# A causal attention layer on one core: masking the keys of each half of the heads on GpSimd in place of VectorE

## What is computed

```
qp = q @ Wq.T ;  kv = latent_kv @ Wkv_expand.T ;  k, v = split(kv)
qh, kh, vh = heads of qp, k, v          # 16 heads of 16 channels
scores = einsum('bhqd,bhkd->bhqk', qh, kh) / sqrt(16)
scores = where(causal, scores, finfo.min)
out = einsum('bhqk,bhkd->bhqd', softmax(scores), vh)
return out @ Wout.T
```

## Time and profile before

| what | us |
|---|---|
| median of 3 runs | 1821.97 (1820.47 to 1822.61) |
| the profiled execution, its own time | 1817.92 |
| its span, first to last instruction | 1816.1 |
| TensorE busy | 1622.1 (89%) |
| VectorE busy | 1230.1 (68%) |
| ScalarE busy | 742.8 (41%) |
| GpSimd busy | 921.1 (51%) |

### The profile page before, as it was taken

The page is one execution under the profiler, slowest core; times in us unless marked ns, Lnnn a source line. Parts: engine busy times, 40 slices in busy tenths (PEclk is TensorE's granted clock), DMA queues, the critical chain, the costliest instruction groups (busy, mean ns, idle before and its releaser), DMA issues. The chain is left out here.

```text
span 1816.1 us, 27644 instructions
## 1 busy us (share of the span) xinstructions
PE 1622.1 (89%) x8770; PEld 1110.5 (61%) x8770; DVE 1230.1 (68%) x2197; ACT 742.8 (41%) x1965; POOL 921.1 (51%) x799
## 2 busy tenths in 40 slices
PE   5999977999999999999999996799999289978980
PEld 4667744555555555555555553499999167665870
DVE  5598768777787777777787744466666757756433
ACT  3100102444444444444444452466666156652220
POOL 0377747777888777777888452023332000000636
PEclk9999987999999999999999997699999699988895
DMA  6434344122212221222212002664444420001443
GB/s 199 134 67 96 69 106 136 42 79 79 79 41 75 79 70 52 79 78 79 79 39 77 10 11 87 211 196 130 132 139 116 156 58 1 0 4 37 123 112 108
DMA packets 91472, 157.41 MB, mean 87 GB/s; under 512 B 45841, under 2 KB 70645, under 8 KB 88077
## 3 DMA queue, kind: packets, MB, share of 16 engines
q1 hardware_dynamic: 84301, 138.86, 26.2%
q0 software_dynamic: 7040, 16.92, 3.2%
HBM read 125.31 MB, written 28.48 MB: 85 GB/s over the span
## 5 line engine op out<-in xcount | busy, mean ns | idle before, releaser
L897 ACT ACTIVATE R<-banks 128x400 f32<-128x400 f32 x768 | 326.7, 509 | 317.9 <-PE banks L931 317.1
L713 DVE TENSOR_REDUCE PM<-banks 128x2 f32<-128x964 f32 x320 | 360.9, 1133 | 137.7 <-PE banks L690 137.6
L751 POOL TENSOR_TENSOR EA<-EA,R 128x400 f32<-128x400 f32 x288 | 306.1, 1063 | 119.2 <-ACT R L897 105.8
L931 PE MATMUL banks<-QS,KH 128*128 128x400 f32 x768 | 288.8, 376 | 2.3 <-DMA QB<-ML 2.3
L931 PE MATMUL banks<-QB,KB 128*128 128x400 f32 x768 | 265.7, 346 | 0.0
L731 DVE TENSOR_TENSOR banks<-banks,R 128x400 f32<-128x400 f32 x320 | 183.8, 574 | 27.9 <-ACT R L897 26.7
L540 POOL TENSOR_TENSOR arena<-arena 96x400 f32<-96x400 f32 x128 | 141.4, 1125 | 115.8 <-DVE arena L515 115.6
L941 PE MATMUL banks<-R,KV 128*64 128x400 f32 x960 | 187.5, 512 | 0.0
L931 PEld LDWEIGHTS banks<-QS,KH 128*128 128x128 f32 x768 | 145.1, 189 | 54.5 <-issue 38.0
L690 PE MATMUL banks<-KH,QS 64*128 64x482 f32 x320 | 160.6, 503 | 17.2 <-DVE PM L713 7.7
L690 PEld LDWEIGHTS banks<-KH,QS 64*128 64x128 f32 x320 | 60.7, 190 | 160.7 <-DVE PM L713 86.4
(11 more groups left out here) (288 smaller groups left out, 3239.0 us busy)
## 6 DMA issues: line engine op xcount, KB each, us to landing
arena<-in_ctx_T SPq DMA_DIRECT2D x16, 1444.0 KB
m_stage_d<-in_m_down SPq DMA_DIRECT2D x32, 672.0 KB
QS<-queries SPq DMA_DIRECT2D x16, 800.0 KB, 6.9
m_up<-in_m_up SPq DMA_DIRECT2D x8, 1392.0 KB, 13.0
queries<-q_out_h SPq DMA_DIRECT2D x64, 100.0 KB, 2.4
queries<-q_out_l SPq DMA_DIRECT2D x64, 100.0 KB, 2.4
QB<-queries SPq DMA_DIRECT2D x16, 400.0 KB, 8.7
arena<-recips SPq DMA_DIRECT2D x32, 200.0 KB
```

The source lines that it names most:

```text
L713: nc.vector.tensor_reduce(PM[:, 2 * i:2 * i + n], banks[:, k:k + n, 0:KW], AX.X, ALU.max).then_inc(red_done, 1)
L751: nc.gpsimd.tensor_tensor(out, first, tile_of(n, 1), ALU.add).then_inc(odd_sum, 1)
L897: nc.scalar.activation(tile_of(n, o), psum[ring_bank(score_tile(b, n, o))][:, 0:CH], ACT.Exp).then_inc(exp_done, 1)
L931: last = nc.tensor.matmul(out, lhs[r][:, keys], heads[:, o], start=lhs is KH, stop=lhs is KB)
```

## The change

The multiplication that masks the keys (before: L2343 on VectorE) is issued by GpSimd, with a semaphore `keys_ready` of its own. GpSimd gets a wait for `s_ready`, the same that `operands` has, since the buffers are unchanged; `operands` keeps its wait and the query copy. TensorE waits for `keys_ready` and `ops_ready` ahead of each half's scores. The operands, shapes, buffers and results of the multiplication are unchanged.

```diff
+        keys_ready = core.sem("cb_keys")
...
                 def scores(i, u):
                     n = i * 2 + u
+                    pe.wait_ge(keys_ready, n + 1)
                     pe.wait_ge(ops_ready, n + 1)
...
+            @block.gpsimd
+            def _(pool):
+                def keys(i, u):
+                    n = i * 2 + u
+                    if has(i, 1, B):
+                        pool.wait_ge(s_ready, n - 1)
+                    nc.gpsimd.tensor_tensor(kb[u][:], KTT[:, u:u + 1, bass.ts(i, S)].to_broadcast([P, HT, S]),
+                                            blocks[:].rearrange("p (h o) -> p h o", o=1).to_broadcast([P, HT, S]),
+                                            ALU.mult).then_inc(keys_ready, 1)
+
+                for i in (0, 1):
+                    for u in range(2):
+                        keys(i, u)
+                with pool.Fori(0, (B - 2) // 2) as j:
+                    for w in range(2):
+                        for u in range(2):
+                            keys(j * 2 + (2 + w), u)
...
                 def operands(i, u):
                     n = i * 2 + u
                     if has(i, 1, B):
                         v.wait_ge(s_ready, n - 1)
-                    nc.vector.tensor_tensor(kb[u][:], KTT[:, u:u + 1, bass.ts(i, S)].to_broadcast([P, HT, S]),
-                                            blocks[:].rearrange("p (h o) -> p h o", o=1).to_broadcast([P, HT, S]), ALU.mult)
                     nc.vector.tensor_copy(qb[u][:], QT[:, u, bass.ts(i, S)]).then_inc(ops_ready, 1)
```

## The result

The changed kernel takes 1826.35 us (median of 17 runs, 1823.69 to 1833.81), the kernel before in the same rounds 1822.34 us (17 runs, 1820.22 to 1825.57). The ratio is 1.0021, with a 95% interval of 1.0011 to 1.0031: slower by 3.8 us, between 2.0 and 5.6. The direction is the one forecast; the forecast of 12.5 us was three times too large.

What follows compares the result with a forecast made beforehand. The prediction took one chain through TensorE, VectorE and ScalarE to bound the attention loop; 11.6 us of late negations plus 0.9 at the start made 12.5 us, so 1834.5 us on the median's footing, range 1821.5 to 1840.

Steps and rivals of the forecast that it cites:

- One chain through three engines: Attention loop: TensorE, VectorE and ScalarE follow one another within 0.2 us, giving the 9.64 us step.
- Taking the masks off VectorE: Attention loop: removing 32 masks of 0.99 us gives nothing back, since all but the first lie beside other work.
- The waits: TensorE's queue, ahead of the scores: 32 more waits, each already met, put at nothing, 2.0 us at most.
- GpSimd holds up the negation: Half 0 of steps 0 to 14: negation 0.77 us late behind GpSimd's mask, 15 x 0.77 = 11.6 us.
- the rate of two elements per cycle: Short VectorE operations within SBUF: about 0.41 ns per element, as if using both SBUF interfaces, one shared with GpSimd.
- the first rival: Loop: one-input VectorE operations are not blocked, only the start's 0.9 us is left, 1823 to 1825 us; chance 0.19.
- the masked form: GpSimd's mask: taken as 1.90 us like a dense 128x800 product, because VectorE needs 0.99 us for both; upper bound 2.85.
- Half 1 is hidden: Half 1's negation is also 0.8 us late, but TensorE needs its tile later, with about 1 us to spare.
- The start: Ahead of the loop's first scores: a mask of 1.90 in place of 0.99 us starts them 0.9 us late.
- The slowdown would not touch TensorE's clock: TensorE's granted clock stays at 1.00, as between 1466 and 1486, where it was busy only 15.19 of 20 us.
- the dearer mask: GpSimd's mask takes 2.85 us, the negation is 1.72 late, 27.7 us in all, so 1850 us; chance 0.08.
- The likeliest case: Whole kernel: negation blocked by a 1.90 us GpSimd mask, 1834.5 us, own range 1831 to 1839; chance 0.69.

Runs made afterwards that it cites:

- dense_second: Changed kernel with only the second operand of GpSimd's multiplication (head mask number repeated over keys) made dense, masking left out: 1835.82 us (one run), step 10.31.
- gated: Changed kernel with GpSimd's masks waiting until VectorE's negation and query copy are over: 1823.58 us, ratio 1.0007 to the kernel before.
- reduce_neg: Changed kernel with the negation made by a one-element reduction with its sign turned, the scale put into the query copy: 1820.72 us, ratio 1.0006 to the kernel before.
- wait_only: Kernel before, masks still on VectorE, plus their own semaphore for which TensorE waits: 1821.67 us, ratio 1.0002 to the kernel before.
- pointer form: Changed kernel with the negation's two numbers read from a small tile: 1826.16 us, ratio 1.0030 to the kernel before; negation 0.50 us.
- dense: Changed kernel with both operands of GpSimd's multiplication replaced by dense 128x800 pieces of the keys' tile, masking left out: 1835.92 us (one run), step 10.21.

## Why the prediction was right in kind and wrong in size

- *One chain through three engines; whatever delays the negation of half 0 lengthens the step one for one.* Right. The negation is 0.33 us longer, ScalarE's wait 0.33, the step 0.32; with 0.68 us lost (dense_second) the step is 0.68 longer; with the collision gone (gated, reduce_neg) it is 9.63 and 9.62.
- *Taking the masks off VectorE gives nothing back.* Right, in the loop as it is (gated: step unchanged) and in the shorter one.
- *The waits cost nothing.* Right (wait_only).
- *GpSimd holds up the negation, for the overlap less 0.14.* Right. The overlap was 1549.11 - 1548.64 = 0.47 us, the loss 0.33. The kernel before had a second overlap in the latent layer, which the prediction didn't use; there VectorE's operation, 0.90 us by itself, lost 0.09 us to an overlap of 387.44 - 387.22 = 0.22:

```profile
386.40 1.04 POOL L751 TENSOR_TENSOR EA<-EA,R 128x400 f32<-128x400 f32 x1 [0.36 <-ACT R L897]
387.22 0.99 DVE L408 TENSOR_TENSOR KB<-arena,KH 64x722 fp32r<-64x722 f32 x1
```

  So overlaps of 0.22, 0.47, 0.66 and 0.82 us cost 0.09, 0.33, 0.52 and 0.68. The reason that I took from the earlier trace rows, the rate of two elements per cycle, is only half supported: the pointer form, which I expected to be free of it, waited too.
- *No row of before has a one-input SBUF-to-SBUF operation under a running GpSimd operation with reads.* Wrong, though nothing in the sum hung on it. In the latent layer a reduction within SBUF (L719, 128x13 from 128x39) runs under GpSimd's L751 or L403, and its 16 executions last 185 to 195 ns. That row spoke for the first rival, and taken alone it would have misled: reduce_neg shows that reductions go free, while the negation, a scalar operation, waits.
- *"On VectorE the masked form costs the same 0.99, so the repeats cost it nothing, and I take 1.90 us for GpSimd too."* This is the step that failed. From VectorE's durations one can't tell what a repeated operand costs GpSimd. There, a number repeated over 100 keys makes the multiplication cheaper, 1.52 us, and I had drawn a bound for dearer (2.85) and none for cheaper. This alone is 0.38 us of a term of 0.77, because the term is a small difference between two large times, GpSimd's end and the negation's start. GpSimd's start, taken as 0.1 behind VectorE's, was 0.04: another 0.06. Then 0.77 - 0.38 - 0.06 = 0.33 us, and the term 15 x 0.77 = 11.6 us measured 5.0. With the mask's time at 1.88 the predicted price came out: the negation of dense_second loses 0.68 us.
- *Half 1 is hidden.* Right: its negation lost as much, and the step grew by half 0's share alone.
- *The start costs 0.9 us.* It was 0.54, for the same reason, the shorter mask.
- *The slowdown would not touch TensorE's clock.* I had said this of the dearer mask, from a stretch of the kernel before. It was no safe reading: in the changed kernel's trace the granted clock fell at the start, which cost 0.61 us there. Whether the masks had a part in it is open.
- In all, 5.0 + 0.5 = 5.5 us by the traces, against 3.8 (2.0 to 5.6) by the runs. The three kernels with a step of 9.95 measured 1.0021, 1.0030 and 1.0040, so the traces' sum is within what the runs say. Whether the rest of the program gave something back in the changed kernel is not shown.
- The whole range, 1821.5 to 1840, held the time, but only because its lower end was drawn for the first rival, whose condition (no blocking) is not what happened; that it held is luck and says nothing for the size of the term. The likeliest case's own, 1831 to 1839, didn't: it had room for GpSimd's start and 0.1 us of the mask's time, but none for a mask of 1.52 us.

## What to carry to other kernels

Before work goes to GpSimd, look at what VectorE does in the microseconds after the same signal. If a copy or scalar operation within SBUF is there and somebody waits for it, expect it to end with GpSimd's operation, as those of 8 and of 100 elements did here; release GpSimd behind it, or make it another kind of operation. And a chain is shortened on the chain: freeing an engine that waits for the others gave nothing here in either form of the loop, while two small operations taken off the chain gave 8 us.

When a cost is the difference between the ends of two overlapping operations, an error in either duration falls on it whole, so both need a bound on each side.

## What the runs showed of the hardware that was not expected

- GpSimd's multiplication of 128 x 800 takes 1.52 us when one operand is a number repeated along the inner dimension, and 1.87 to 1.90 us when both are dense there; a repeat of the other operand along the outer dimension saves nothing (dense_second against dense). VectorE takes 0.98 to 0.99 us either way.
- A scalar operation on 8 elements whose two numbers come from a tile takes 0.29 us instead of 0.17, and loses only 0.21 us under a mask in which the plain one loses 0.33: both end 0.03 us behind GpSimd, as if the 0.12 us that the pointer form takes longer by itself had passed under the wait.
- TensorE's granted clock fell to its lower level at the start of the loop in some executions (for 3.4 us in the changed kernel's, for 6.8 in wait_only's) and not in others, with the masks on either engine.
